# A gated cross-attention block of four stages: the last pair's third and fourth stages as two chains by batch, its gated tiles over four PSUM banks, and new orders of all engines

## What is computed

```python
def _L0_xattn_ref(KEY, VALUE, QUERY, ...):            # first attention
    k, q, v = heads(KEY @ Wk_w.T + Wk_b), heads(QUERY @ Wq_w.T + Wq_b), heads(VALUE @ Wv_w.T + Wv_b)
    score = jnp.einsum('bhij,bhkj->bhik', k, q) / jnp.sqrt(dh)
    attn = jax.nn.softmax(score, axis=1)              # over the 16 heads
    out = jnp.einsum('bhik,bhij->bhjk', attn, v)
    return merge(out) @ Wo_w.T + Wo_b

def _L0_ffn_ref(x, gate_kernel, w0_kernel, w1_kernel, wo_kernel):   # 8 experts, top 2
    weights = scatter(softmax(top_k(x @ gate_kernel, 2)))
    layer_mult = jax.nn.silu(einsum('ble,neh->blnh', x, w0_kernel)) * einsum('ble,neh->blnh', x, w1_kernel)
    intermediate = jnp.einsum('blnh,nhe->blne', layer_mult, wo_kernel)
    return jnp.einsum('blne,bln->ble', intermediate, weights)

def _L1_xattn_ref(c, q, w_cq, b_cq, w_c, b_c, w_q, b_q, W_l, b_l):  # second attention
    s = (c @ w_c + b_c)[:, :, None] + (q @ w_q + b_q)[:, None, :] + einsum('bcd,bqd,d->bcq', c, q, w_cq) + b_cq
    a = jax.nn.softmax(s, axis=2)
    c2q_att = jnp.einsum('bcq,bqd->bcd', a, q)
    b_att = jax.nn.softmax(jnp.max(s, axis=2), axis=1)
    q2c_att = jnp.einsum('bc,bcd->bd', b_att, c)[:, None, :]
    return concatenate([c, c2q_att, c * c2q_att, c * q2c_att]) @ W_l.T + b_l

def _L1_ffn_ref(x, w_gate, w_up, w_down):             # activations to 8 bits, weights to -1, 0, 1
    gate = jax.nn.silu(_bitlinear(x, w_gate))
    return _bitlinear(gate * _bitlinear(x, w_up), w_down)

x = x + jnp.tanh(g_xattn[0]) * _L0_xattn_ref(ctx_1024, ctx_1024, _layernorm(x), ...)
x = x + jnp.tanh(g_ffn[0]) * _L0_ffn_ref(_layernorm(x), ...)
x = x + jnp.tanh(g_xattn[1]) * _L1_xattn_ref(_layernorm(x), ctx_1024, ...)
x = x + jnp.tanh(g_ffn[1]) * _L1_ffn_ref(_layernorm(x), ...)
```

## Time and profile before

| | us |
|---|---|
| median of 3 executions | 431.16 |
| lowest, highest | 428.95, 432.51 |
| the profiled execution, its own time | 426.3 |
| its span in the trace | 424.5 |
| PE, DVE, ACT, POOL busy in it | 314.2, 333.7, 236.7, 282.5 |
| mean granted TensorE clock | 0.931 |

### The profile page before, as it was taken

The page is one execution under the profiler, slowest core; times in us unless marked ns, Lnnn a source line. Parts: engine busy times, 40 slices in busy tenths (PEclk is TensorE's granted clock), DMA queues, the critical chain, the costliest instruction groups (busy, mean ns, idle before and its releaser), DMA issues. The chain is left out here.

```text
span 424.5 us, 9867 instructions
## 1 busy us (share of the span) xinstructions
PE 314.2 (74%) x3074; PEld 274.4 (65%) x3074; DVE 333.7 (79%) x1013; ACT 236.7 (56%) x632; POOL 282.5 (67%) x435
## 2 busy tenths in 40 slices
PE   0322469797898799889986997889687988994722
PEld 0211258686797688678965896778566887983611
DVE  2279777698889999988898989897898788786143
ACT  3434145336736684668557846675456757745433
POOL 4448979779698979695978797958586844321110
PEclk9999999998999999959999999899989999995565
DMA  4956311311122112211203130114000000000000
GB/s 124 286 178 191 93 32 39 94 39 34 30 91 64 33 43 76 64 46 43 79 1 107 46 101 1 32 51 121 13 14 2 28 11 2 26 13 2 11 2 13
DMA packets 34435, 24.14 MB, mean 57 GB/s; under 512 B 3600, under 2 KB 32080, under 8 KB 34384
## 3 DMA queue, kind: packets, MB, share of 16 engines
q1 hardware_dynamic: 33664, 23.32, 18.4%
q10 hardware_dynamic: 720, 0.20, 0.2%
HBM read 16.16 MB, written 7.34 MB: 55 GB/s over the span
## 5 line engine op out<-in xcount | busy, mean ns | idle before, releaser
L1077 PE MATMUL ps_z<-m_xhi,w_hi 128*128 128x256 f32 x256 | 84.7, 331 | 13.0 <-DVE m_xlo L1446 5.8
L876 POOL TENSOR_TENSOR attn<-attn,head_inv 128x1024 f32<-128x1024 f32 x32 | 75.6, 2368 | 1.0 <-DVE head_inv L1442 0.9
L1078 PE MATMUL ps_z<-m_xhi,w_lo 128*128 128x256 f32 x256 | 75.5, 295 | 0.0
L1079 PE MATMUL ps_z<-m_xlo,w_hi 128*128 128x256 f32 x256 | 75.2, 294 | 0.0
L955 ACT ACTIVATE m_tanh<-ps_z 128x256 f32<-128x256 f32 x128 | 49.0, 383 | 46.5 <-PE ps_z L1079 44.8
L1296 PE MATMUL ps_d<-wdn,m_h 128*128 128x128 f32 x512 | 70.4, 280 | 4.6 <-DVE m_h L1467 2.5
L1296 PEld LDWEIGHTS ps_d<-wdn,m_h 128*128 128x128 f32 x512 | 62.2, 191 | 8.6 <-DVE m_h L1467 4.5
L1077 PEld LDWEIGHTS ps_z<-m_xhi,w_hi 128*128 128x128 f32 x256 | 51.8, 202 | 22.0 <-DVE m_xlo L1446 7.4
L1459 DVE SCALAR_TENSOR_TENSOR m_u<-m_tanh,ps_z 128x256 f32<-128x256 f32 x128 | 52.7, 414 | 13.0 <-ACT m_tanh L955 10.1
L823 POOL TENSOR_TENSOR m_h<-m_u,m_z 128x256 f32<-128x256 f32 x56 | 41.1, 733 | 25.0 <-DVE m_u L1459 24.3
L1078 PEld LDWEIGHTS ps_z<-m_xhi,w_lo 128*128 128x128 f32 x256 | 52.2, 204 | 0.0
(11 more groups left out here) (244 smaller groups left out, 751.1 us busy)
## 6 DMA issues: line engine op xcount, KB each, us to landing
rows_dram<-qk_parts SPq DMA_DIRECT2D x16, 192.0 KB, 2.3
k_rows<-rows_dram SPq DMA_DIRECT2D x16, 192.0 KB
q_rows<-rows_dram SPq DMA_DIRECT2D x16, 192.0 KB
w_raw<-in_w SPq DMA_DIRECT2D x2, 1024.0 KB, 6.9
rows_dram<-qk_parts SPq DMA_DIRECT2D x16, 128.0 KB, 2.0
x_in<-in_x SPq DMA_DIRECT2D x8, 128.0 KB, 2.1
ct_in<-in_ctx_t SPq DMA_DIRECT2D x8, 128.0 KB, 2.5
rows_dram<-qk_parts SPq DMA_DIRECT2D x16, 64.0 KB, 1.6
```

The costliest lines, as they stand in the source:

```text
L876: pool.tensor_tensor(e, e, head_inv[:, u % 2].unsqueeze(1).to_broadcast([P, HEADS, HALF]), ALU.mult).then_inc(s_attn, 1)
L1077: pe.matmul(dst, hi_w, hi_x, start=start, stop=False)
L1078: pe.matmul(dst, lo_w, hi_x, start=False, stop=False)
L1079: return pe.matmul(dst, hi_w, lo_x, start=False, stop=True)
```

## The change

For the last pair alone the third stage is cut into two chains, one per batch. `groups(p)` is `((0, 1),)` for pairs with a successor, which keeps their instructions as they were, and `((0,), (1,))` for the last; steps loop over it, and `late_bank` puts all third-stage results of the last pair's second batch into `ps_a`. The wait for x1 of the second batch, which frees `ps_a`, moves from z to the transposes of `f_c`. From `f_ct` to `x3` each step then has two instructions of half size, each with its own wait. In the fourth stage `g_q`, the transpose and `g_qt` are cut too, and the final store is two stores of 64 KB. Layer norms (`f_stats`, `g_stats`, `f_norm`, `g_norm`) and `g_amax` to `g_r` stay whole, so `g_stats` waits for both `x3`.

The last pair's 16 gated tiles go round the four banks `ps_z0`, `ps_z1`, `ps_sc0`, `ps_sc1` (`tile_banks`), so that PE may write tile k when tile k-4 has been read, and no longer k-2.

All numbers of `WHEN` and `ONCE` are new. Of the two numbers for a step one line is shown. The diff, cut to its core (the steps left out are changed in the way of the ones shown):

```diff
-    "act.f_norm": (9833, 13739, 17962, 22386, 26752, 31223, 34780, 37964),
+    "act.f_norm": (9839, 13837, 18058, 22349, 26669, 30861, 34439, 37639),
...
-    "sp.w_out": 106,
+    "sp.w_out": 12,
...
+def groups(p):
+
+    return ((0, 1),) if p.after() else ((0,), (1,))
+
+
+def cols(g):
+
+    return slice(g[0] * P, (g[-1] + 1) * P)
+
+
+def both(g):
+
+    return slice(g[0], g[-1] + 1)
...
-        def z_bank(p, b):
+        def late_bank(p, b):
 
             return ps_a if b and not p.after() else ps_f
...
+        def tile_banks(p):
+
+            return (ps_z[0], ps_z[1]) if p.after() else (ps_z[0], ps_z[1], ps_sc[:, 0], ps_sc[:, 1])
+
+        def tile_bank(p, k):
+
+            return tile_banks(p)[k % len(tile_banks(p))]
...
-                    sp.wait_ge(s_o, p.count(2, 2))
-                    sp.dma_start(o_d[p.rows()].rearrange("o s b d -> s (o b) d"), o_sb[:]).then_inc(stored, 16)
-            sp.wait_ge(stored, 16 * PAIRS)
+                    for g in groups(p):
+                        sp.wait_ge(s_o, p.count(2, g[-1] + 1))
+                        sp.dma_start(o_d[p.rows()].rearrange("o s b d -> s (o b) d")[:, both(g)],
+                                     o_sb[:, both(g)]).then_inc(stored, 16)
+            sp.wait_ge(stored, 16 * (PAIRS + 1))
...
                 if p := due(now, "act.g_qt"):
-                    act.wait_ge(s_gqt, p.count(1, 1))
                     wait(act, s_gu, p.before().count(4, 4))
-                    act.activation(g_qt[:], ps_g[:, 0:P].bitcast(BF16), ACT.Copy).then_inc(s_gqs, 1)
+                    for g in groups(p):
+                        act.wait_ge(s_gqt, p.count(1, 1) + g[0])
+                        act.activation(g_qt[:, cols(g)], batch_bank(p, g[0])[:, g[0] * HALF:(g[-1] + 1) * HALF].bitcast(BF16),
+                                       ACT.Copy).then_inc(s_gqs, 1)
...
                 if p := due(now, "pe.f_c2q"):
-                    pe.wait_ge(s_fats, p.count(1, 1))
-                    pe.wait_ge(s_fe, p.count(4, 4))
-                    for b in range(2):
-                        pe.matmul(ps_f[:, b * P:(b + 1) * P], ctx_in[:, b], f_at[:, b * P:(b + 1) * P],
-                                  start=True, stop=True)
-                    for b in range(2):
-                        last = pe.matmul(ps_f[:, TOK + b:TOK + b + 1], f_c[:, b], f_e[:, b:b + 1],
-                                         start=True, stop=True)
-                    last.then_inc(s_fq, 1)
+                    for g in groups(p):
+                        pe.wait_ge(s_fats, p.count(1, 1) + g[0])
+                        pe.wait_ge(s_fe, p.count(4, 2 * g[-1] + 2))
+                        for b in g:
+                            pe.matmul(late_bank(p, b)[:, b * P:(b + 1) * P], ctx_in[:, b], f_at[:, b * P:(b + 1) * P],
+                                      start=True, stop=True)
+                        for b in g:
+                            last = pe.matmul(late_bank(p, b)[:, TOK + b:TOK + b + 1], f_c[:, b], f_e[:, b:b + 1],
+                                             start=True, stop=True)
+                        last.then_inc(s_fq, 1)
...
                 if p := due(now, "pe.f_z", 0):
-                    pe.wait_ge(s_fc2, p.count(1, 1))
-                    pe.wait_ge(s_fq2, p.count(1, 1))
                     if p.first:
                         pe.wait_ge(w_late, 32)
-                    if not p.after():
-                        pe.wait_ge(s_x1, p.count(2, 2))
-                    for b in range(1 if p.after() else 2):
+                    for g in groups(p):
+                        b = g[0]
+                        pe.wait_ge(s_fc2, p.count(1, 1) + b)
+                        pe.wait_ge(s_fq2, p.count(1, 1) + b)
                         s = slice(b * P, (b + 1) * P)
-                        pe.matmul(z_bank(p, b)[:, s], f_ct[:, s], wl[:, 0], start=True, stop=False)
-                        pe.matmul(z_bank(p, b)[:, s], f_c2q[:, s], wl[:, 1], start=False, stop=False)
+                        pe.matmul(late_bank(p, b)[:, s], f_ct[:, s], wl[:, 0], start=True, stop=False)
+                        pe.matmul(late_bank(p, b)[:, s], f_c2q[:, s], wl[:, 1], start=False, stop=False)
                 if p := due(now, "pe.f_z", 1):
-                    pe.wait_ge(s_fpr, p.count(1, 1))
-                    pe.wait_ge(s_fw, p.count(2, 2))
-                    for b in range(2):
-                        s = slice(b * P, (b + 1) * P)
-                        if b and p.after():
-                            pe.matmul(z_bank(p, b)[:, s], f_ct[:, s], wl[:, 0], start=True, stop=False)
-                            pe.matmul(z_bank(p, b)[:, s], f_c2q[:, s], wl[:, 1], start=False, stop=False)
-                        pe.matmul(z_bank(p, b)[:, s], f_prod[:, s], wl[:, 2], start=False, stop=False)
-                        last = pe.matmul(z_bank(p, b)[:, s], f_ct[:, s], f_w4[:, b], start=False, stop=True)
-                    last.then_inc(s_fz, 1)
+                    for g in groups(p):
+                        pe.wait_ge(s_fpr, p.count(1, 1) + g[0])
+                        pe.wait_ge(s_fw, p.count(2, g[-1] + 1))
+                        for b in g:
+                            s = slice(b * P, (b + 1) * P)
+                            if b and p.after():
+                                pe.matmul(late_bank(p, b)[:, s], f_ct[:, s], wl[:, 0], start=True, stop=False)
+                                pe.matmul(late_bank(p, b)[:, s], f_c2q[:, s], wl[:, 1], start=False, stop=False)
+                            pe.matmul(late_bank(p, b)[:, s], f_prod[:, s], wl[:, 2], start=False, stop=False)
+                            last = pe.matmul(late_bank(p, b)[:, s], f_ct[:, s], f_w4[:, b], start=False, stop=True)
+                        last.then_inc(s_fz, 1)
...
-                        pe.wait_ge(s_gqs, p.count(1, 1))
+                        pe.wait_ge(s_gqs, p.count(1, 1) + (0 if p.after() else b))
                         if p.first and u == 0:
                             pe.wait_ge(c_wr, 5)
                         if p.after():
                             wait(pe, s_gp, p.count(4, u))
-                        elif u < 2:
-                            pe.wait_ge(s_exp, p.count(4, 4))
                         else:
-                            wait_product(pe, p, TILES - 4 + u)
...
-                        elif b == 0:
-                            pe.wait_ge(s_gqs, p.count(1, 1))
                         else:
-                            pe.wait_ge(s_y, p.count(2 * EXPERTS, 2 * EXPERTS))
+                            pe.wait_ge(s_gqs, p.count(1, 1) + b)
                         for k in range(NI):
                             last = pe.transpose(batch_bank(p, b)[:, k * HALF:(k + 1) * HALF].bitcast(BF16),
...
-                        wait(pe, s_mu, p.count(TILES, k - 1))
-                        r = (k - 2) % TILES
-                        q = p.before() if k < 2 else p
-                        if r in POOL_TILES:
-                            wait(pe, s_z1, q.count(len(POOL_TILES), POOL_TILES.index(r) + 1))
+                        back = 2 if k < 2 else len(tile_banks(p))
+                        if k < back and k >= 2:
+                            pe.wait_ge(s_shift, p.count(4, 4))
                         else:
-                            wait(pe, s_mh, q.count(len(DVE_TILES), DVE_TILES.index(r) + 1))
+                            wait(pe, s_mu, p.count(TILES, k - back + 1))
+                            r = (k - back) % TILES
+                            q = p.before() if k < back else p
+                            if r in POOL_TILES:
+                                wait(pe, s_z1, q.count(len(POOL_TILES), POOL_TILES.index(r) + 1))
+                            else:
...
                 if p := due(now, "dve.g_stats"):
-                    dve.wait_ge(s_x3, p.count(1, 1))
+                    dve.wait_ge(s_x3, p.count(1, 1) + len(groups(p)) - 1)
...
                 if p := due(now, "dve.x3"):
-                    dve.wait_ge(s_fz, p.count(1, 1))
                     dve.wait_ge(s_fyb, p.count(1, 1))
                     wait(dve, s_o, p.before().count(2, 2))
-                    if p.after():
-                        dve.scalar_tensor_tensor(x3[:], ps_f[:, 0:TOK].rearrange("p (b d) -> p b d", b=2), th[:, 1:2],
-                                                 y_res[:], ALU.mult, ALU.add).then_inc(s_x3, 1)
-                    else:
-                        dve.scalar_tensor_tensor(x3[:, 0], ps_f[:, 0:P], th[:, 1:2], y_res[:, 0], ALU.mult,
-                                                 ALU.add)
-                        dve.scalar_tensor_tensor(x3[:, 1], ps_a[:, P:TOK], th[:, 1:2], y_res[:, 1], ALU.mult,
-                                                 ALU.add).then_inc(s_x3, 1)
+                    for g in groups(p):
+                        dve.wait_ge(s_fz, p.count(1, 1) + g[0])
```

(7 more changed lines are left out.)

406 lines of the change are left out of this document (217 added, 189 removed), and 272 rows, old and new, of the table WHEN.

## The result

The changed kernel is faster by about twice what was forecast. In the first measurement its median is 418.72 us (4 executions, 417.74 to 424.90) against 430.06 for the kernel before (4 executions, 428.67 to 432.51); the ratio is 0.972, with a 95% interval of 0.966 to 0.979. The forecast was 426.8, with a range that began at 421.5. Medians are taken over all executions, ratios and their intervals only over those within 1.5% of the fastest of their kernel, so the two need not agree. Of one kernel, single executions lie over 10 us apart, so one comparison alone says little of a microsecond. The traces say more, since a chain in them repeats to some hundredths.

What follows compares the result with a forecast made beforehand. DVE bounds the six middle pairs, PE close behind; the end is a chain of single instructions. End -2.7, banks -1.0, start 0, middle -0.7 sum to -4.4: 426.8 us against the median 431.16, own range 424 to 430, wider range 421.5 to 433.

Steps and rivals of the forecast that it cites:

- the start: First loads, K product and scores: later bias work and an earlier q fetch give 0, from -1.5 to +2.5 us.
- the middle: Up to the last pair: half of DVE's 1.33 us wait before that pair's first scores goes, -0.7 us, from -1.3 to 0.
- the end: From 383 us on: third stage -1.5, fourth stage -0.8, last store -0.4, together -2.7 us.
- Rival B: Middle pairs: the new orders also save a tenth of DVE's idle 41.65 us, 4.2 us, giving 423.3; chance 0.18.
- Four banks: Last pair's tiles: two tiles more of room let PE run ahead of DVE, -1.0 us, from 0 to -2.0.
- The two moves on ACT: Last pair's third stage: g_tanh ahead of f_c costs 0.6, g_pr ahead of f_erow 0.5, together +1.1 us.
- What the cut regains: Last pair's third-stage chain: every second handing-on by batch saves half a small link, -1.1 us, up to the c2q products.
- The idle 1.11 ahead of z: PE's block of g_pq transposes and z products starts when the c2q products end, without the idle time: -1.2 us.
- g_q and g_qt by batch: Last pair's fourth stage, g_r to first up product: the first batch goes ahead, -0.8 us, from 0 to -1.1.
- The last store: End of the run: a final store of 64 KB and not 128 lands sooner, -0.4 us, from 0 to -0.7.
- The clock, left at half: PE's z block in the last pair's third stage: TensorE's clock stays at half, so no gain was counted.
- rival E: The clock opens in the z block: 1.6 us less, giving 425.2; chance 0.03.

Runs made afterwards that it cites:

- start_new: The changed kernel's code with the new orders only for the first some 28 us, then those of before: median 423.35 us, ratio 0.993 to the kernel before.

## Why the prediction was right and wrong

It was right in direction and in what the change does: a gain in the end's chain, a smaller one from the banks, and a wait on ACT that is made longer. It was wrong in size: 4.4 us forecast, 9.4 to 12.6 between medians, and 418.7 outside the range. Three terms of the sum were too small: the start (0, measured -1.6), the middle (-0.7, measured -2.3, and not by the wait that was named for it) and the end (-2.7, measured -4.5, most of all what the cut by batch regains). By its own steps:

- **The start, taken at 0**, within -1.5 to +2.5: it is -1.6 at the first pair's m_st (means of nine and eight traces). The first head maximum does come at the same time as before (28.6 and 28.7), as forecast. The gain arises behind it, up to the first pair's m_st. start_new keeps it up to the last pair, once executions are compared at equal clock. Which instruction behind the first head maximum comes sooner was not followed up.
- **The middle, -0.7**: at equal clock -2.3 by the two lines. The bound of 4 us for unknown orders held. Rival B, the new orders helping the middle, was the right one in kind with 0.18, and its 423.3 was still too high. The step that failed is that a term was taken only where a row showed a wait, and everything else in the middle was put at 0: that wait, 1.33 us and to be halved, stayed (1.32), and the gain came from elsewhere. From which waits is open.
- **Four banks, -1.0**: -0.8 (34.12 to 33.34), with the two-bank run at 34.19. Right in size; 0.4 of it is shown to be the banks' (34.19 to 33.8 in the old order), the other 0.4 came only with the new orders.
- **The two moves on ACT, +1.1**: the sum came near, its parts didn't. f_c did start 0.56 late, as forecast with 0.6, but in the chains by batch the scores behind it start only 0.09 late, since they stand behind the fourth g_up on PE in either order. g_pr ahead of f_erow costs 0.7 and not 0.5. Together that is 0.84. With the third stage whole the new orders cost 1.04, and there the scores start 0.6 late (3.77 against 3.18): the cut hides f_c's delay. g_pmax on DVE, a move that the prediction didn't name, costs 0.7 only when f_c is put back.
- **What the cut regains, -1.1**: it is -1.9 to -2.1 (13.19 to 11.29 in the old orders, 14.23 to 12.13 in the new). This is the term that was most undersized in the end. I reckoned that every second handing-on saves half a small link, and the two bounds reached only twice that; in the old orders the lead grows at each of the five marks, by 0.1, 0.2, 0.5, 0.5 and 0.5.
- **The idle 1.11 ahead of z, -1.2**: the block started 0.14 before the last c2q product ended, 1.25 better against it than before. Right. The block kept its length, 4.6, and x3's 0.30 went to 0.04. Together the third stage gave -2.60, forecast -1.5 with -2.6 as the far bound.
- **g_q and g_qt by batch, -0.8**: -0.46, or -0.66 against the run with them whole.
- **The last store, -0.4**: -1.0 to -1.35 against before, but -0.2 to -0.3 against the two traces with one store. The Trainium skill (DMA: Bandwidth & Descriptors, Anatomy of one DMA) has a transfer's fixed part not depend on its bytes; it says so of the gpsimd path, these stores go out on SP, and the traces agree with it: 1.8 us to landing for 128 KB and 1.6 for 64 KB. The size that the prediction reckoned with was not what made the end of before longer. There the landing took 2.6 to 2.9 us, with a packet of the instruction queue in it; whether that is the cause is open.
- **The clock, left at half**: rival E happens, and not by the change alone. In the z block the clock opened part of the way in five traces, the changed kernel's second (0.57 over the third stage, block 3.6 long) and one of the kernel before among them (x3 at 19.18 in place of 19.59). It is worth up to 1.0 us (block of 3.6 and not 4.6) in one execution and none in another. Why it opens in some is open.
- **The frame.** The forecast was for the median of three executions, 431.16, which the medians of 11 and 17 executions, 426.7 to 430.2, show to be a long sample. The profile from which the terms were read was of a short execution (426.3).

Added up from means of the traces: start -1.6, middle at equal clock -2.3, the last pair's second stage -0.8, and from its f_st to the end -4.8 (before 41.8, 41.4 and 41.0; after 37.3, 36.0 and 36.6): -9.5. The medians have -11.3, -9.4 and -12.6. The comparison of all executions at equal clock has 9.6. What the medians have beyond that, up to 3 us, goes with the clock: 31.0 us lost in the mean over the executions of before, 25.4 over the changed kernel's, of which the shorter end is 3.4. That the new orders make stretches at half clock rarer isn't shown: the seven other kernels with the new middle lost 28.0 in the mean of 45 executions, the four with the new code and the old middle 28.2 in 39.

## What to carry to other kernels

Cut the last work of a pipeline into independent chains even where each half costs more than half: the end has idle engines, and almost every handing-over gains. When an engine's list is reordered there, ask of every step that was moved past another one whether the chain's next step is already waiting behind it, and what stands behind its waiter in the other engine's queue. The costly move here was a g_pr of 0.80 us ahead of an f_erow that was ready; a late reduction of 0.68 us on DVE cost nothing until another move was undone. A move can hide another's cost, so undo them one by one. And compare marks in traces at equal clock, not medians, where one program varies by more than the change is worth.

## What of the hardware was not expected

- One program on one core varied from 421.35 to 435.5 us, and the larger part of it follows the time at half clock: 0.7 to 0.8 us for each us of clock lost between the marks, 0.6 over whole executions (three quarters of the variance of the 69 of before). Three executions lay far beyond, each of another kernel: 460.7 (before, mean clock 0.741), 485.3 (start_new, 0.675) and 530.5 us (the fourth stage whole, 0.605).
- Stretches at half clock in the middle begin mostly near the same few places (about 100, 132, 182, 265 and 300 to 325 us), but not all of them come up in each execution; where PE was busy 1.95 of 4 us (before, from 180 us) the clock fell and stayed at half while it was then busy 4.00 of 4. The Trainium skill (TensorE: Matmul & The Clock Gate, What's actually happening) has sustained activity release the throttle; the two windows at 184 and 188 us agree only in that the clock was full again just past 192 (0.97 in 192 to 196).
- A chain of single instructions repeats to 0.02 us from chip to chip: from g_r to the first up product 1.66 or 1.67 in all thirteen traces with the cut, 2.13 in three of three before.
